# Row maxima in a row take the scores' banks in turn, with other tasks between them; one token mixing of the last layer is issued after the last products with V

## The reference, cut to what matters

```python
    latent_kv = x @ w_kv_down
    kv = latent_kv @ w_kv_up
    ...
    q = (x @ w_q).reshape(Bx, Tx, N_HEAD, HEAD_SIZE)
    att = jnp.einsum('bqhd,bkhd->bhqk', q, k) * scale
    att = jnp.where(causal, att, -jnp.inf)
    att = jax.nn.softmax(att, axis=-1)
    y = jnp.einsum('bhqk,bkhd->bqhd', att, v)
    y = y.reshape(Bx, Tx, HD)
    return y @ w_out
    ...
    xr = mu_r * x + (1.0 - mu_r) * x_prev
    xk = mu_k * x + (1.0 - mu_k) * x_prev
```

## Time and profile before

| | |
|---|---|
| median of 3 runs | 2138.2 us (2132.14 to 2140.27) |
| the profiled execution's own time | 2138.73 us |
| its span in the profile | 2137.4 us |
| granted TensorE clock, mean | 0.977 of 2.4 GHz |
| busy: PE, DVE, ACT, POOL | 92%, 63%, 51%, 67% |
| attention's steady part | about 400 to 1960 us |

### The profile page before, as it was taken

The page is one execution under the profiler, slowest core; times in us unless marked ns, Lnnn a source line. Parts: engine busy times, 40 slices in busy tenths (PEclk is TensorE's granted clock), DMA queues, the critical chain, the costliest instruction groups (busy, mean ns, idle before and its releaser), DMA issues.

```text
span 2137.4 us, 34866 instructions
## 1 busy us (share of the span) xinstructions
PE 1974.2 (92%) x12720; PEld 1223.4 (57%) x12720; DVE 1347.1 (63%) x2719; ACT 1100.0 (51%) x2234; POOL 1426.1 (67%) x812
## 2 busy tenths in 40 slices
PE   4999568999999999999989999999999999999899
PEld 3666445555555555556555665555556555555466
DVE  4888646576657565766655657576656575656443
ACT  4776634445444444445455454445454445454575
POOL 0343314778687868786858687868787878687822
PEclk9999779999999999999999999999999999999999
DMA  3000000000000000000000000000000000000001
GB/s 122 1 1 1 0 7 6 20 11 17 12 20 11 17 11 20 12 17 13 18 11 17 11 20 11 17 12 19 11 18 11 20 12 17 11 14 11 25 25 60
DMA packets 29242, 36.99 MB, mean 17 GB/s; under 512 B 6928, under 2 KB 20368, under 8 KB 29072
## 3 DMA queue, kind: packets, MB, share of 16 engines
q1 hardware_dynamic: 29072, 34.76, 5.3%
HBM read 30.02 MB, written 4.46 MB: 16 GB/s over the span
## 4 chain that ended last, share of the span: by engine, by line
PE 60%; DVE 16%; POOL 13%; ACT 6%; issue 5%; DMA 0%; POOLq 0%; ACTq 0%; DVEq 0%; SPq 0%
PE heads_out L878 16%; POOL acc L1372 11%; PE beside L695 9%; PE two_heads L834 7%; PE scores L695 6%; PE scores L857 4%; PE scores L863 4%; PE scores L859 4%; PE scores L861 4%; DVE part_max L1070 3%; ACT prob L1287 2%; PE beside L889 2%; DVE stats L917 2%; PE two_heads L695 2%; DVE wQK_lo L1031 1%
## 5 line engine op out<-in xcount | busy, mean ns | idle before, releaser
L1372 POOL TENSOR_TENSOR acc<-acc,prob 128x1024 f32<-128x1024 f32 (+3 forms) x512 | 1018.2, 1989 | 207.4 <-ACT prob L1287 151.8
L1287 ACT ACTIVATE prob<-scores 128x512 f32<-128x512 f32 (+3 forms) x1280 | 579.4, 539 | 641.3 <-PE scores L863 290.2
L1070 DVE TENSOR_REDUCE part_max<-two_heads 128x2 f32<-128x1024 f32 x384 | 469.4, 1222 | 279.0 <-PE two_heads L834 278.3
L878 PE MATMUL heads_out<-prob,V 128*64 128x512 f32 (+3 forms) x2560 | 544.3, 546 | 0.0
L1067 DVE CUSTOM_DVE_ANT_0 two_heads<-two_heads,mask 128x128 f32<-128x128 f32 (+3 forms) x512 | 242.2, 515 | 187.2 <-PE two_heads L834 187.1
L834 PE MATMUL two_heads<-k_hi,q_hi 64*128 64x512 f32 (+3 forms) x1280 | 274.6, 424 | 63.9 <-DVE part_max L1070 34.0
L878 PEld LDWEIGHTS heads_out<-prob,V 128*64 128x64 f32 x2560 | 156.8, 137 | 233.4 <-issue 210.4
L834 PEld LDWEIGHTS two_heads<-k_hi,q_hi 64*128 64x128 f32 x1280 | 121.0, 185 | 256.7 <-issue 130.8
L857 PE MATMUL scores<-q_hi,k_hi 64*128 64x512 f32 (+3 forms) x1280 | 236.7, 365 | 1.6 <-ACT neg_max L1274 0.8
L859 PE MATMUL scores<-q_hi,k_lo 64*128 64x512 f32 (+3 forms) x1280 | 235.6, 363 | 0.0
L863 PE MATMUL scores<-neg_max,sel 64*128 64x512 f32 (+3 forms) x1280 | 235.6, 362 | 0.0
(11 more groups left out here) (299 smaller groups left out, 2911.8 us busy)
## 6 DMA issues: line engine op xcount, KB each, us to landing
rden<-rden_rows SPq DMA_DIRECT2D x128, 128.0 KB, 2.9
X<-u SPq DMA_DIRECT2D x8, 512.0 KB, 9.0
out<-X SPq DMA_DIRECT2D x8, 512.0 KB, 2.9
wQK_raw<-wQuery SPq DMA_DIRECT2D x16, 192.0 KB, 2.9
wO_raw<-wOut SPq DMA_DIRECT2D x16, 128.0 KB, 2.8
wV_raw<-wValue SPq DMA_DIRECT2D x8, 128.0 KB, 2.7
den<-den_rows SPq DMA_DIRECT2D x64, 4.0 KB
rden_rows<-den SPq DMA_DIRECT2D x64, 4.0 KB, 1.3
```

Source lines behind the costliest of these rows:

```text
L878: made = pe.matmul(heads_out[head(h), x0:], V[vn % NVS][:, tt, p % 2, head(h)], prob[step % NPROB][:, h, x0:], start=t == 0, stop=t == TPB ...
L1070: made = ve.reduce_max(part_max[:, t, :, c:c + 1], two_heads[:, :, 0:width], AX.X)
L1287: ac.activation(prob[step % NPROB][:, h, x0:], bank(task, h)[:, x0:], ACT.Exp).then_inc(empty(task, h)[0], 1)
L1372: po.tensor_tensor(total[:, :, x0:], total[:, :, x0:], new[:, :, x0:], ALU.add).then_inc(acc_ok, 1)
```

## The change

Four edits. (1) A `maximum` whose predecessor among the tasks that take a bank is also a `maximum` takes the next of three pairs of banks, (5, 6), (0, 1), (2, 3); after any other such task it starts again at (5, 6). `weigh` takes no bank in this sense, so two maxima with only weighs between them count as in a row. (2) In the loop that catches up on maxima, a filler is put behind each. (3) `mix_tokens` of block 1 of the last mixing goes from 6 steps ahead of the end of the scores to behind the last `weigh`. (4) The matmul and the reductions look up their banks (`two_banks`).

```diff
-        self.side_bank = 7
+        self.side_bank, self.max_banks = 7, 0
...
         elif kind == "maximum":
-            self.take(task, (5, 6))
+            before = next((x[0] for x in reversed(self.tasks[:-1]) if x in self.bank), None)
+            self.max_banks = (self.max_banks + 1) % 3 if before == kind else 0
+            self.take(task, ((5, 6), (0, 1), (2, 3))[self.max_banks])
...
-                 -6: [("mix_tokens", "b", 1)], -4: [("turn_normal", "b", 2)]}
+                 -4: [("turn_normal", "b", 2)], 0: [("mix_tokens", "b", 1)]}
...
             while self.at < goal - 1:
                 maximum()
+                filler(10 ** 6)
...
+        def two_banks(task):
+
+            first = plan.bank[task][0][0][0]
+            return two_heads[:, :, :] if first == 5 else scores[:, first:first + 2, :]
...
-                        made = pe.matmul(two_heads[:, h, 0:width], q[head(h), t * P:(t + 1) * P], k[head(h), 0:width], start=True, stop=True)
+                        made = pe.matmul(two_banks(task)[:, h, 0:width], q[head(h), t * P:(t + 1) * P], k[head(h), 0:width], start=True, stop=True)
...
-                            made = ve.tensor_tensor_reduce(out=two_heads[:, h, 0:width], in0=two_heads[:, h, 0:width], in1=mask[:, BLK - width:], scale=1.0,
-                                                           scalar=MASKED, op0=ALU.add, op1=ALU.max, accum_out=part_max[:, t, h, c:c + 1])
+                            scored = two_banks(task)[:, h, 0:width]
+                            made = ve.tensor_tensor_reduce(out=scored, in0=scored, in1=mask[:, BLK - width:], scale=1.0, scalar=MASKED, op0=ALU.add, op1=ALU.max, accum_out=part_max[:, t, h, c:c + 1])
                     else:
-                        made = ve.reduce_max(part_max[:, t, :, c:c + 1], two_heads[:, :, 0:width], AX.X)
+                        made = ve.reduce_max(part_max[:, t, :, c:c + 1], two_banks(task)[:, :, 0:width], AX.X)
```

## The result

The changed kernel takes 2203.8 us (median of six runs, 2201.7 to 2209.9) against 2138.3 us for the kernel before: a ratio of 1.0316, 95% interval 1.0296 to 1.0335. The forecast was 2181 us in a range of 2158 to 2203. The direction was right; the size was not: the loss is 65.5 us in the medians where 42.7 was forecast, and the median lies 0.8 us above the range. The profiled execution is the slowest of the six, 2209.92 us, 71.2 above the profiled one of before. It has the lowest granted clock of the six, 0.970 against 0.971 to 0.975. The terms further down add up to its 71.2.

What follows compares the result with a forecast made beforehand. PE, busy 92% of the span, was taken to bound the kernel. Steady part 51.7, start of attention -8 + 5 and end -6 sum to 42.7 us on 2138.7: forecast 2181 us, range 2158 to 2203.

Steps and rivals of the forecast that it cites:

- the pairs: Seven places with two moved maxima, the first waited for before: 1.5 us lost each, 10.5 us, between 6 and 18.
- the start of attention: Units 1 to 4: -8 us from waits taken away, +5 us from moved maxima ahead of scores.
- Places ahead of scores: Steady part: scores wait for reductions in their own banks; 20 full-width places 31.0 us, 14 masked ones 12.2 us.
- the rival of the falling clock: Clock falls to 0.50 in the stalls: 12 us more at 7 pairs, 80 at all 48 places; chance 0.06.
- Start of attention, the loss: Seven moved maxima of units 2 to 4 put a reduction's wait ahead of scores: +5 us, between 3 and 8.
- Start of attention, the gain: Reduction waits go or shrink, first maximum of unit 2 about 6 us earlier: -8 us, between -3 and -11.
- End of attention: Moved mixing takes away PE's 3.11 us wait and about 3 us of half clock: -6 us, between -3 and -8.
- What POOL covers: Steady part: POOL, running later than PE in 10 of 14 units, hides 0.2 us per unit: -2.0 us.
- Half made up: Rival: other engines work on during PE's stalls, leaving 26 of 51.7 us in the steady part: 2155 us; chance 0.12.
- turning pays: Rival: scores find reductions done or PE regains the stall, so moved maxima only lose waits: 2121 us; chance 0.04.

Runs made afterwards that it cites:

- The experiment with other banks: Changed kernel, but the second of two maxima in a row takes banks 2 and 3 first, not 0 and 1: 2156.8 us, 1.0082 to the kernel before.
- the experiment that differs in these seven alone: Changed kernel with only the nine moved maxima of units 1 to 4 turned, none later: 2137.3 us, ratio 1.0010 to the kernel before.
- no turning: Changed kernel with all maxima back in banks 5 and 6, filler and moved mixing kept: 2132.9 us, ratio 0.9965 to the kernel before.
- turning alone: Changed kernel with banks turning, but no filler in the loop and mixing in its old place: 2200.3 us, ratio 1.0290 to the kernel before.
- the mixing alone: Kernel before with only the last mixing operations moved, banks and loop unchanged: 2133.9 us, ratio 0.9976 to the kernel before.
- the pairs alone: Only the seven pairs of maxima turn; no filler in the loop, mixing in its old place: 2158.1 us, ratio 1.0100 to the kernel before.
- all maxima ahead of scores: From unit 6 on, 294 maxima go into banks 0 and 1; no loop filler, mixing in its old place: 2567.8 us, 1.2024 to the kernel before.
- only the first two turned: Changed kernel with only unit 1's third and fourth maxima turned, filler and moved mixing kept: 2124.7 us, ratio 0.9956 to the kernel before.
- the last experiment 288 waits: 288 counts waits; the run is all maxima ahead of scores, 294 in banks 0 and 1: 2567.8 us, ratio 1.2024 to the kernel before.

## Why the prediction was right and wrong

The mechanism was right, the scores' wait for a reduction in their own banks. Two terms of the sum failed: the pairs and the start of attention. Of the 28.5 us by which 71.2 exceeds 42.7, the pairs are 10.5 and the start 12.9 (+9.9 where -8 + 5 was forecast); the end is 2.8, POOL 2.0, the single places 1.7, and -1.4 lies elsewhere. Both failed terms lie outside their own bounds. The step behind some 15 of these 23 us is that the clock would hold: the sum has nothing for it, and its fall stood beside the sum as a rival at 0.06. The rest is mostly the second maximum of a pair and the gain at the start. Another 5.7 us, the distance from 65.5 to 71.2, are the profiled execution's own.

*Places ahead of scores: right.* 1.55 and 0.87 were forecast, 1.60 and 0.92 measured on average, at all 34 places. The 0.1 for PE's restart and the 0.05 for the signal stood in the prediction without a row. Unit 22 bears both out: the scores start 1.83 - 0.34 = 1.49 us later and what follows them some 1.6, and they start 0.06 after the reduction's end (876.46 + 1.23 = 877.69). The experiment with other banks bears out that it is the wait.

*Pairs: mis-sized, 10.5 forecast, 21.0 measured.* In the four pairs with no half clock the first maximum costs 0.5 to 0.8 us, near the 0.5 of the forecast, and the second 1.60, where 1.0 was forecast; seven such pairs would be 15.9. The timeline of the changed kernel at unit 7, the place of the earlier trace rows:

```profile
475.62 0.50 PE L842 MATMUL scores<-k_hi,q_hi 64*128 64x512 f32 x2 [0.44 <-ACT prob L1295]
477.44 0.39 PE L865 MATMUL scores<-q_hi,k_hi 64*128 64x256 f32 x2 [1.32 <-DVE part_max L1078]
...
478.42 0.44 PE L842 MATMUL two_heads<-k_hi,q_hi 64*128 64x512 f32 x2
...
480.44 0.50 PE L842 MATMUL scores<-k_hi,q_hi 64*128 64x512 f32 x2
482.27 0.50 PE L865 MATMUL scores<-q_hi,k_hi 64*128 64x512 f32 x2 [1.32 <-DVE part_max L1078]
```

At the first, the 0.74 us that (7, 1, 2) waited for DVE did not go altogether: 0.44 came back as a wait for ACT, which had not yet read the scores in banks 0 and 1. I had looked only at who reads banks 5 and 6. The second is the step that failed: (7, 2, 0) had no wait before that could be used. That it started at 467.56, just when a reduction ended, was no wait, for the weighs held PE until 467.49, and its row shows no idle time. Before:

```profile
465.77 1.72 PE L878 MATMUL heads_out<-prob,V 128*64 128x512 f32 x8
467.56 0.51 PE L834 MATMUL two_heads<-k_hi,q_hi 64*128 64x512 f32 x2
```

So it costs what a single full-width place costs. And the clock falls at three pairs, 5.1 us more, 1.7 each. This is the rival of the falling clock, with the price that it gave to a stretch; I had held it to all seven pairs or all 48 places.

For unit 39, the pair with windows of the changed kernel ahead of the fall, in it and behind it:

```profile
1364.00:1367.00 3.00, 1.49 (x20) 1.21 (x20) 2.03 (x4) 0.81 (x3) 2.65 (x2) 1.00 0.00 0
1367.00:1371.00 4.00, 4.00 (x16) 1.08 (x13) 1.90 (x3) 1.51 (x5) 3.44 (x3) 0.57 0.25 69
1371.00:1374.00 3.00, 1.67 (x16) 1.27 (x16) 1.23 (x1) 0.22 (x1) 2.53 (x3) 1.00 0.02 5
```

*Start of attention, the loss: near in the sum of the waits, wrong in the clock.* The step that seven moved maxima of units 2 to 4 put the same wait ahead of scores, +5, left the clock out; the experiment that differs in these seven alone has 13.0. From just ahead of unit 1's first scores to just ahead of unit 3's, 72.2 us before and 84.7 after, the two kernels' windows read, before:

```profile
325.11:397.33 72.22, 60.50 (x401) 36.51 (x402) 43.92 (x90) 30.19 (x63) 38.36 (x20) 1.00 0.03 10
```

and after, with PE's waits for reductions in it:

```profile
322.49:407.20 84.71, 70.30 (x397) 42.88 (x398) 42.46 (x89) 30.40 (x62) 38.35 (x20) 0.86 0.03 9
```

```profile
PE scores L865 <- DVE part_max L1078: 6.7, 3, 2.8
PE scores L865 <- DVE part_max L1076: 5.2, 4, 2.3
PE two_heads L842 <- DVE part_max L1078: 1.2, 2, 0.8
```

These waits are 13.1 us; before they were 8.9 in ten, so 4.2 more, close to the 5. As a wait of 1.7 us for transposes went, PE is idle only 2.7 us longer. The other 9.8 of the 12.5 us are the same matmuls at a clock of 0.86: PE is busy that much longer for them. I had argued from one stretch at full clock behind a wait of 1.32 us that the clock would hold; here single waits reach 2.8 us, where I had put 1.1. The reason is in the order of DVE: a moved maximum no longer waits for the one ahead of it, so their two reductions stand in a row, and the scores wait for both at once. In the changed kernel, maximum (3, 1, 2):

```profile
364.58 1.23 DVE L1078 TENSOR_REDUCE part_max<-two_heads 128x2 f32<-128x1024 f32 x1
365.72 1.22 DVE L1078 TENSOR_REDUCE part_max<-scores 128x2 f32<-128x1024 f32 x1
...
366.99 0.80 PE L865 MATMUL scores<-q_hi,k_hi 64*128 64x512 f32 x2 [1.78 <-DVE part_max L1078]
```

The Trainium skill, TensorE: Matmul & The Clock Gate, section A second HAM failure mode: psum-queue depth-cycling, tells of a kernel that turns through PSUM banks with short idle times of PE between its groups, and whose clock goes up and down with them. The trace agrees at the start and in three pairs. At the 34 single places of the changed kernel the waits of 0.7 and 1.3 us left no half clock; with 294 places some of them did.

*Start of attention, the gain: too large, and hard to size.* -8 was forecast (-3 to -11); the scores of unit 1 come 2.6 us earlier in the changed kernel, 3.3 with no turning, 4.0 with turning alone. The first maximum of unit 2, forecast 6 us earlier, starts at 313.30 us in place of 316.4, 3 earlier: the query and the key of unit 2 are 6 to 7 us ahead, but the maximum before them, (1, 1, 3), now behind more matmuls on PE, is 2 us late. The kernel before is also the fastest of four executions with one order here: the first scores of unit 3 start at 397.6 us in it and at 399.6 to 400.2 with the mixing alone, the pairs alone and all maxima ahead of scores. With no turning and with only the first two turned they start at 394.0 and 394.5, so the gain is 3.0 to 6.2 us.

*End of attention: right in the wait, the size not known well.* The wait of 3.11 us is gone in all kernels that move the mixing. Against the one profiled execution of the kernel before they gain 5.3 to 6.9 us there in five traces, and 3.2 in the changed kernel's:

```profile
2102.04 0.55 PE L703 MATMUL beside<-wO_hi,oT_hi 128*128 128x256 f32 x1 [3.09 <-DVE oT_lo L1113]
...
2103.59 3.68 PE L886 MATMUL heads_out<-prob,V 128*64 128x512 f32 x8
```

Here the half clock comes right behind the wait for `oT_lo`, and eight matmuls of the weighs take 3.68 us (1.94 at full clock). Before, the same wait of 3.10 us left the clock up, and it fell behind the second one. But two kernels that leave the mixing in its place gain at the end as well, 1.0 us (turning alone) and 3.7 (the pairs alone), with the clock falling elsewhere. With the pairs alone it fell during the weighs ahead of that wait, and the wait for X shrank without the move:

```profile
2048.28 3.59 PE L885 MATMUL heads_out<-prob,V 128*64 128x512 f32 x8
...
2053.34 0.39 PE L702 MATMUL beside<-wO_hi,oT_hi 128*128 128x256 f32 x1 [1.47 <-DVE X L1120]
```

So a part of the 5.3 to 6.9 is where the clock fell, and not the move. The times of the mixing alone, 2.6 to 7.7 us, are the better measure; the forecast of 6 lies within, and so does 3.2.

*What POOL covers: nothing.* All 14 units with two places paid in full. The 0.2 us by which POOL was the later one at unit 22 hid nothing; the chain that ran over POOL in 10 of these units before runs over it in none after.

*Half made up, and turning pays: both out.* Nothing of the stalls is seen to come back, at 48 places or at 294. By the Trainium skill's rule on turning banks that the prediction weighed (Perfetto Trace Analysis, Optimizing Tensor Performance), turning would pay; the runs show that it does not where the bank is that of the very next group. In 0 and 1 a full-width place costs 1.60 us and a masked one 0.92; in 2 and 3, whose scores come 0.92 us later, 0.67 and nothing.

## What to carry to other kernels

A buffer that looks free for the writer is judged by who writes it next: if that is the very next task, the reader of the buffer moves onto the path, however idle the reader's engine is. Price such a wait by a place in the same trace where the same pair of tasks already shares a buffer, here 1.81 us from the earlier trace rows, and ask also who read the new buffer last, which here was ACT. Before a wait is taken as removed, see from its row that it is a wait and not an engine busy until the same moment. And before a few microseconds are put down to an edit, see how far executions of one order lie apart: here 2.7 us at the start of attention, and 3.7 at its end.

## What the runs showed of the hardware

The granted clock did not follow the sum of the stalls alone. In the last experiment 288 waits of 355.5 us in all, 18% of the time from 460 to 2450 us, left it at 0.97; 13.1 us of waits in 85 us at the start, 15%, went with 0.86. At the start it fell behind single waits of 1.8 to 2.8 us. Of the seven pairs two or three brought a fall, behind the first maximum's wait of 1.32 us, and not the same ones in three kernels; units 15 and 63, whose first maximum does not wait for ACT ahead of it, show none in any of them, which no run tests. Behind a single 1.32 us at the 20 full-width places of the changed kernel it never fell; with 294 places, where such waits lie some 6 us apart, it fell in 27 stretches. Executions of one order differ in where it falls. What decides stays open.
